# One decoder kernel, stage cross0: bf16 pairs for the norms' sums, split by POOL, and another order of its projections

## The reference, cut to what matters

```python
def rmsnorm(x, g, eps=EPS):
    var = jnp.mean(jnp.square(x), axis=-1, keepdims=True)
    return x * jax.lax.rsqrt(var + eps) * g
```

## Time and profile before

| what | before |
|---|---|
| median of 3 runs | 2926.01 us (2922.60 to 2928.53) |
| the profiled execution | 2923.55 us |
| its span | 2921.70 us |
| granted TensorE clock, mean | 0.945 |
| PE busy | 2509.2 us (86% of the span) |
| DVE busy | 1862.7 us (64%) |
| ACT busy | 1572.5 us (54%) |
| POOL busy | 864.7 us (30%) |

### The profile page before, as it was taken

One profiled execution on the slowest core, in us unless ns is written; L12 is line 12 of the kernel. 1 busy time (PEld: TensorE's weight loads), 2 busy tenths in 40 slices (PEclk: granted clock), 3 DMA queues, 4 the chain that ended last, 5 costly groups with the idle time before them and its releaser, 6 DMA issues. The chain is left out here.

```text
span 2921.7 us, 60581 instructions
## 1 busy us (share of the span) xinstructions
PE 2509.2 (86%) x21768; PEld 1612.3 (55%) x21768; DVE 1862.7 (64%) x3317; ACT 1572.5 (54%) x2742; POOL 864.7 (30%) x741
## 2 busy tenths in 40 slices
PE   6888888888888898888978999989999999986454
PEld 4555555455655565566455666655566666643222
DVE  4666663366665666666155666651688888858886
ACT  4666663176766666666043555550577777732321
POOL 4556555400110010012232212223100000146675
PEclk9999998999999999999988999999999999998777
DMA  3333333144444444446230333341477777852000
GB/s 96 71 71 92 68 73 81 47 89 92 97 95 91 95 91 96 93 94 124 80 151 21 85 88 87 88 94 46 84 146 145 143 151 145 153 115 77 20 0 29
DMA packets 752867, 263.39 MB, mean 90 GB/s; under 512 B 724816, under 2 KB 724816, under 8 KB 751184
## 3 DMA queue, kind: packets, MB, share of 16 engines
q1 hardware_dynamic: 750960, 255.48, 41.0%
q0 software_dynamic: 1760, 5.77, 0.7%
HBM read 82.84 MB, written 2.10 MB: 29 GB/s over the span
## 5 line engine op out<-in xcount | busy, mean ns | idle before, releaser
L786 ACT ACTIVATE ph<-p,ri 128x1024 bf16<-128x1024 f32 (+4 forms) x512 | 437.4, 854 | 461.6 <-DVE ri L1056 394.9
L1066 DVE SCALAR_TENSOR_TENSOR pl<-p,ri,ph 128x1024 bf16<-128x1024 f32 (+4 forms) x512 | 517.4, 1010 | 129.6 <-issue 83.5
L1122 PE MATMUL ps<-wo_hi,v_hi 128*128 128x128 bf16 x2688 | 487.2, 222 | 79.4 <-DMA wo_lo<-pl 79.3
L1123 PE MATMUL ps<-wo_lo,v_hi 128*128 128x128 bf16 x2688 | 487.0, 222 | 0.0
L1124 PE MATMUL ps<-wo_hi,v_lo 128*128 128x128 bf16 x2688 | 486.9, 222 | 0.0
L797 ACT ACTIVATE p<-p,nb 128x1024 f32<-128x1024 f32 (+4 forms) x512 | 435.7, 851 | 48.4 <-DVE nb L1049 33.9
L1122 PEld LDWEIGHTS ps<-wo_hi,v_hi 128*128 128x128 bf16 x2688 | 266.7, 99 | 142.9 <-DMA wo_lo<-pl 96.0
L1122 PE MATMUL ps<-k_hi,q_hi 128*128 128x512 bf16 (+3 forms) x768 | 277.2, 361 | 45.9 <-issue 30.1
L1123 PEld LDWEIGHTS ps<-wo_lo,v_hi 128*128 128x128 bf16 x2688 | 266.9, 99 | 39.1 <-issue 0.8
L1124 PE MATMUL ps<-k_hi,q_lo 128*128 128x512 bf16 (+3 forms) x768 | 277.1, 361 | 0.0
L1123 PE MATMUL ps<-k_lo,q_hi 128*128 128x512 bf16 (+3 forms) x768 | 276.9, 361 | 0.0
(11 more groups left out here) (197 smaller groups left out, 6066.4 us busy)
## 6 DMA issues: line engine op xcount, KB each, us to landing
raw_kv<-in_wkvself SPq DMA_DIRECT2D x32, 512.0 KB, 3.9
raw_q<-in_wqself SPq DMA_DIRECT2D x32, 256.0 KB, 2.7
wo_hi<-ph SPq DMA_TRANSPOSE x512, 3.1
wo_lo<-pl SPq DMA_TRANSPOSE x512, 3.1
raw_q<-in_woself SPq DMA_DIRECT2D x32, 256.0 KB, 2.8
raw_q<-in_wqcross SPq DMA_DIRECT2D x32, 256.0 KB, 2.7
raw_q<-in_wocross SPq DMA_DIRECT2D x32, 256.0 KB, 3.0
raw_kv<-in_wkvcross SPq DMA_DIRECT2D x24, 256.0 KB, 3.1
```

Of the source, the lines that this page charges most:

```text
L786: nc.scalar.activation(m["ph"][:, qt % 2, 0:w], m["p"][:, qt % 2, 0:w], ACT.Copy, scale=ri[:, qt % 2:qt % 2 + 1]).then_inc(p_norm, 1)
L1066: nc.vector.scalar_tensor_tensor(out=m["pl"][:, qt % 2, 0:w], in0=m["p"][:, qt % 2, 0:w], scalar=ri[:, qt % 2:qt % 2 + 1], in1=m["ph"][:, ...
L1122: nc.tensor.matmul(o, l(0), r(0), start=first, stop=False)
L1123: nc.tensor.matmul(o, l(0), r(1), start=False, stop=False)
```

## The change

1. The plan of jobs: K0 | K1, KN0 | Q, KN1 | QN, V0, V1, where it was K0 | KN0, K1 | KN1, Q | QN, V0, V1.
2. POOL splits each square into a bf16 pair `sqs` (`split_squares`: a rounding, then a subtraction), and the sums become bf16 matmuls over both halves with `onesb`. ACT waits for POOL's subtraction before it overwrites `sq`; POOL waits for the sum that read the pair before.
3. VectorE copies QN's sums directly behind the scores of step 3, ahead of the remainder; the head's output comes behind the jobs' rows on both ACT and VectorE.
4. ACT makes the key norms in step 3 between the wait for that step's scores and its exponential, where it made them at the end of step 2.

```diff
@@ Layer.jobs
-            plan = [[("K", 0)], [("KN", 0), ("K", 1)], [("KN", 1), ("Q", 0)], [("QN", 0), ("V", 0), ("V", 1)]]
+            plan = [[("K", 0)], [("K", 1), ("KN", 0)], [("Q", 0), ("KN", 1)], [("QN", 0), ("V", 0), ("V", 1)]]
@@ POOL
+                def split_squares(n, it, qt, jobs):
+
+                    for kind, half in jobs:
+                        if kind not in ("K", "Q"):
+                            continue
+                        s = 2 if kind == "Q" else half
+                        count = lambda n: c["sq"] + 3 * (n + 1) + s + 1
+                        pool.wait_ge(sq_ok, at(count, n, it))
+                        if n >= 0 or s:
+                            pool.wait_ge(job_mm, at(lambda n: c["job"] + squares_free(n, s), n, it))
+                        pool.nop(nofuse=True)
+                        nc.gpsimd.tensor_scalar(m["sqs"][0][:, :], m["sq"][:, :], 1.0, 1.0, ALU.mult, ALU.mult).then_inc(sq_hi, 1)
+                        pool.wait_ge(sq_hi, at(count, n, it))
+                        pool.nop(nofuse=True)
+                        nc.gpsimd.tensor_tensor(m["sqs"][1][:, :], m["sq"][:, :], m["sqs"][0][:, :], ALU.subtract).then_inc(sq_lo, 1)
+
+                def squares_free(n, s):
+
+                    return L.before(n - 1, 3) + 1 if s == 0 else L.before(n, 1) + 2 if s == 1 else L.before(n, 2) + 2
@@ POOL unit
                         if L.rms:
+                            split_squares(n, it, qt, L.jobs(n, qt))
                             query_norms(n, it, qt, L.jobs(n, qt))
@@ ACT job_parts
                             if L.rms:
+                                s = 2 if kind == "Q" else half
+                                act.wait_ge(sq_lo, at(lambda n: c["sq"] + 3 * (n + 1) + s, n, it))
                                 nc.scalar.activation(m["sq"][:, :], bank, ACT.Square).then_inc(sq_ok, 1)
@@ ACT unit
                         prob = m["p"][:, qt % 2, 0:L.width(qt)]
+                        if L.rms and qt == QT - 1:
+                            key_norms(n, it, qt - 1, L.jobs(n, qt - 1))
...
+                        job_parts(n, it, qt, L.jobs(n, qt))
                         if qt == QT - 1 and n:
                             heads_out(n - 1, it)
-                        job_parts(n, it, qt, L.jobs(n, qt))
                         if L.rope and qt > 0:
                             rotated(n, it, qt - 1, L.jobs(n, qt - 1))
-                        if L.rms:
-                            key_norms(n, it, qt, L.jobs(n, qt))
@@ DVE unit
                         scores(n, it, qt)
+                        job_parts(n, it, qt, L.jobs(n, qt), ("QN",))
                         if n or qt:
                             remainder(*prior)
+                        job_parts(n, it, qt, L.jobs(n, qt), ("K", "KN", "Q", "V"))
                         if qt == QT - 1 and n:
                             heads_out(n - 1, it)
-                        job_parts(n, it, qt, L.jobs(n, qt))
@@ PE job
                     elif kind == "KN":
-                        pe.wait_ge(sq_ok, at(lambda n: c["sq"] + 3 * (n + 1) + half + 1, n, it))
-                        last = nc.tensor.matmul(bank, ones[:, :], m["sq"][:, :], start=True, stop=True)
+                        pe.wait_ge(sq_lo, at(lambda n: c["sq"] + 3 * (n + 1) + half + 1, n, it))
+                        nc.tensor.matmul(bank, onesb[:, :], m["sqs"][0][:, :], start=True, stop=False)
+                        last = nc.tensor.matmul(bank, onesb[:, :], m["sqs"][1][:, :], start=False, stop=True)
                     elif kind == "QN":
-                        pe.wait_ge(sq_ok, at(lambda n: c["sq"] + 3 * (n + 1) + 3, n, it))
+                        pe.wait_ge(sq_lo, at(lambda n: c["sq"] + 3 * (n + 1) + 3, n, it))
                         for q in range(QT):
-                            last = nc.tensor.matmul(bank[:, q:q + 1], m["sq"][:, q * P:q * P + P], ones[:, 0:1], start=True, stop=True)
+                            nc.tensor.matmul(bank[:, q:q + 1], m["sqs"][0][:, q * P:q * P + P], onesb[:, 0:1], start=True, stop=False)
+                            last = nc.tensor.matmul(bank[:, q:q + 1], m["sqs"][1][:, q * P:q * P + P], onesb[:, 0:1], start=False, stop=True)
                     last.then_inc(job_mm, 1)
```

More of the change, by code:

```diff
@@ L137, in build @@
         ones = sb("ones", [P, P], F32)
+        onesb = sb("onesb", [P, P], BF16)
         idx = sb("idx", [P, IT], I32)
@@ L152, in build @@
         job_mm, job_hi, job_lo = sem("job_mm"), sem("job_hi"), sem("job_lo")
-        sq_ok, k_log, k_norm, q_norm = sem("sq_ok"), sem("k_log"), sem("k_norm"), sem("q_norm")
+        sq_ok, sq_hi, sq_lo, k_log, k_norm, q_norm = sem("sq_ok"), sem("sq_hi"), sem("sq_lo"), sem("k_log"), sem("k_norm"), sem("q_norm")
         rope_sum, rope_hi, rope_lo = sem("rope_sum"), sem("rope_hi"), sem("rope_lo")
@@ L279, in build @@
                 m["sq"] = sb("sq", [P, S], F32, s)
+                m["sqs"] = [sb(f"sq_{k}", [P, S], BF16, s) for k in hl]
                 m["rk"] = sb("rk", [P, 2, SC], F32, s)
@@ L458, in _ @@
             nc.gpsimd.tensor_scalar(idb[:, :], ident[:, :], 1.0, 1.0, ALU.mult, ALU.mult).then_inc(idb_ok, 1)
+            nc.gpsimd.tensor_scalar(onesb[:, :], ones[:, :], 1.0, 1.0, ALU.mult, ALU.mult).then_inc(idb_ok, 1)
             def split_hi(hi, src):
@@ L619, in _ @@
                     if L.rms:
+                        split_squares(-1, None, qt, L.jobs(-1, qt))
                         query_norms(-1, None, qt, L.jobs(-1, qt))
@@ L982, in _, with job_parts @@
                     continue
-                def job_parts(n, it, qt, jobs):
+                def job_parts(n, it, qt, jobs, kinds=("K", "KN", "Q", "QN", "V")):
                     u = n + 1
                     for x, (kind, half) in enumerate(jobs):
+                        if kind not in kinds:
+                            continue
                         bank = ps[:, M_BANK + (L.before(n, qt) + x) % 2, :]
@@ L1297, in unit @@
                             weigh(bn, it, bq)
+                if L.rms:
+                    pe.wait_ge(idb_ok, 2)
                 pe.wait_ge(x_lo, c["ln"] + NT)
```

## The result

The changed kernel takes 2877.65 us (median of 4 runs, 2876.55 to 2878.89) against 2924.31 us before, a ratio of 0.984 (95% interval 0.983 to 0.986): 47 us or 1.6% faster. The profiled execution has a span of 2877.1 us, 44.6 less than before. Of these, 44.4 lie between scores 0 of unit 0 and scores 0 of unit 31: 593.98 to 1328.89, 734.91 us where it was 779.35.

The account below looks back on a forecast made before the run. Bound: VectorE-ACT loop in steps 0 and 1, TensorE's V1 hole in step 3. 31 x 22.58 plus 22.0 at boundaries is 722 against 779.35, 57 less; prologue 2 more, so 55 less: 2871 us, range 2848 to 2905.

Parts of the forecast that it names:

- rk on the loop: Step 1: VectorE copies row rk after K1's low half, adding 0.61 to the two-engine loop, 5.23 instead of 4.62.
- Q behind K1's low half: Step 2: Q uses K1's bank and waits some 0.8 us on TensorE for K1's low half.
- Sum 0: First key-norm sum on TensorE: waits 1.27 us for POOL's subtraction, with 1.05 in hand before scores 2.
- QN: Q's norm sums on TensorE: wait 0.24 us for POOL, then take 0.45 as bf16 instead of 0.81.
- the hole: Step 3: TensorE's wait before V1 for nq to free QN's bank; 2.44 us a unit would go.
- The boundaries: Six loop turns: extra wait of first scores falls from 4.93 to 3.67 each, 29.6 to 22.0 us in all.
- the 1.26 in hand: End of step 3: TensorE would have the next scores 0 ready at 21.3 of 22.58 us.
- 13.9: Stage time in us put down to some nine units with the clock lowered behind the V1 wait; taken as gone.
- A: Rival: TensorE alone sets the pace, 20.06 us a unit, 128 us less, 2798; chance 5%.
- B: Rival: little gain is left, loop additions cost 1.0 to 1.8 us more per unit, 2897 to 2926; chance 14%.
- C: Rival: scattered TensorE idling lowers the clock, 24.86 us a unit, 13 us slower, 2939; chance 8%.
- splits and remainders would not meet: POOL's splits and VectorE's remainders run at different times, nothing added; if every split met one, 9 us.

Follow-up runs that it names:

- nq early: The kernel before with only VectorE's copy of QN's sums moved directly behind scores 3; 2845.3 us, ratio 0.973.
- pairs in the old plan: The kernel before with QN's sums copied directly behind scores 3 and POOL's bf16 pairs, old plan of jobs; 2882.7 us, ratio 0.987.
- new plan and head's output last: The changed kernel with ACT's key norms back at the end of step 2; 2866.6 us, ratio 0.980.
- POOL's longer split: The changed kernel with one more rounding of 0.7 us on POOL ahead of each split; 2885.6 us, ratio 0.989.
- pairs alone: The kernel before with only POOL's split and bf16 sums, old plan and old row order; 2991.9 us, ratio 1.023.
- both old: The changed kernel with QN's copy back behind the remainder and the head's output back ahead of the jobs' rows; 3038.7 us, ratio 1.040.

## Why the prediction was right

**The unit.** Forecast 4.62 + 5.23 + 5.45 + 7.28 = 22.58, measured 4.62 + 5.21 + 5.48 + 7.31 = 22.62. Each term shows in its place: rk on the loop (0.60), Q behind K1's low half (0.63 of wait, forecast some 0.8), scores 3 waiting 0.34 for TensorE, the key norms ahead of the exponential. Sum 0 waits 1.09 (forecast 1.27), QN 0.18 (0.24). QN itself was taken at 0.45 and takes 0.21; lying in TensorE's slack, that moved nothing. Walking one unit queue by queue, with pitches and not durations, gave the unit to 0.2%.

**The parts.** The units of four kernels make a ladder from before to after: nq early 23.74 to 21.28, -2.46; pairs in the old plan to 22.39, +1.11; new plan and head's output last to 21.89, -0.50; key norms late to 22.62, +0.73. The forecast had the hole at 2.44 and said that most of what TensorE gives up goes back into the loop. What it did not say, though its own terms did, is that the first edit alone would be the better kernel.

**The boundaries** are the term that was mis-sized. "At a boundary the 1.26 in hand is used first: 6 x 3.67 = 22.0": measured 28.7, 4.78 each. The slack was there and was used: from the last of the scores' matmuls to scores 0 there are 1.99 us in a plain unit and 0.95 at the boundary shown. But the 4.93 that it was taken from did not stay. In the kernel before, the second hole at the same turn was short and stood behind the scores' matmuls, where scores 0 do not wait for it:
```profile
1018.96 0.60 PE L1122 MATMUL ps<-k_hi,q_hi 128*128 128x512 bf16 x1 [3.38 <-issue]
...
1022.09 0.39 PE L1122 MATMUL ps<-cT_hi,wkv_hi 128*128 128x512 bf16 x1 [0.40 <-issue]
```
In the changed kernel it stands in front of the last of them at all six turns, and is 1.27 to 1.92 us long. Why it moved there is not known. "I take the 13.9 as gone too" was mis-sized as well. Those 13.9 were not all behind the V1 hole: of the nine long units of the kernel before, six stood right behind a boundary, and in three of the nine the low clock was what was left of the boundary's own stretch. The three inside a turn or behind the loop are gone, and the 15 units that come two or more behind a boundary stand at 22.54 to 22.62; the six right behind a boundary stay long, with 6.0 us in all. Together 12.7 us of the 12.9 by which the stage missed its 722.

**Luck.** The median came out 6.7 us above the forecast, and not 12.9, for reasons that the prediction did not have. Up to the stage's first scores the run grew by 0.8 us instead of the 2 forecast (the prologue itself, from K0's first low half on, by 0.4), what follows the stage was 1.0 us shorter, and the profiled execution of the changed kernel lies 1.2 us above its median where that of the kernel before lay 2.5 below.

**The rivals.** A (TensorE alone sets the pace, 20.06): the unit went to 22.62, and even with the hole shut and nothing added it stays at 21.19 to 21.28. B did not happen: POOL's longer split moves no unit. C did not happen in the changed kernel (0.97 granted over 600 to 1290 us, as before), but pairs alone and both old show that it can, at 0.93 and 0.90.

**POOL and VectorE.** The forecast that splits and remainders would not meet holds: all 96 subtractions of the squares take 1.15 to 1.16. Others met. The timeline of POOL in the changed unit:
```profile
1050.91 0.62 POOL L464 TENSOR_SCALAR wq_hi<-raw_q 128x512 bf16<-128x512 f32 x1
...
1059.09 1.16 POOL L598 TENSOR_TENSOR sq_lo<-sq,sq_hi 128x512 bf16<-128x512 f32 x1
...
1061.75 1.99 POOL L582 TENSOR_TENSOR nq<-nq,half_neg 128x4 f32<-128x4 f32 x1 [0.38 <-DVE nq L1028]
```
The power of nq, four elements wide, takes 1.99 us here and took 1.01 in the kernel before, where it ran beside VectorE's copy of a bank: now the remainder runs from 1061.59 for 1.27. The Trainium skill, GPSIMD Engine Reference, Key points, states that POOL contends with VectorE instructions that have two SBUF inputs, and the trace agrees for this one as well. It cost nothing, for the power is due 3.9 us later.

## What to carry to other kernels

When an engine waits for a bank, look at where the row that frees it stands in its own queue before making work cheaper: one copy of 0.16 us moved ahead of two rows gave 79 us, the whole change that contains it 47. A helper engine may take over work only with its latency in hand at the consumer: the same pairs cost 1.1 us a unit where the sum was due at once and saved 0.4 where one or two other jobs stood between. And an edit that looks free because another one made room should be timed alone: the key norms' new place cost 0.73 a unit.

## What the runs showed of the hardware that was not expected

- A remainder on VectorE took 1.58 us instead of 1.28 when a rounding on POOL, started 0.11 earlier (1050.91 beside 1051.02), ran with it: the contention goes both ways. In seven units of the changed kernel it is these 0.30, in seven more about 0.42, once 0.97 (2.25 at 1312.38, beside a subtraction that started with it); for POOL up to 0.98. In the kernel before, all remainders of the stage took 1.28 to 1.29.
- TensorE's loop turn costs more than its hole: 3.0 us without instructions, a second hole of 1.27 some 2.3 us later, and the 1.2 GHz level over the matmuls between. Written out, cross0 with its 32 units was 37 us (changed) and 46 us (nq early) shorter; the other attention stages, written out all together, gained nothing.
- A bf16 weight load of 128 x 128 with a matmul of one column behind it has a pitch of 0.026 us (eight in 0.21), half of the 0.056 of a load and a matmul with 128 columns, from which the estimate of 0.45 was made.
- Whether the clock falls behind a hole depends on more than the hole: one of 2.2 to 2.3 us, the same in every unit, was followed by a fall in six of 31 units before, and one of 2.5 us in most units of pairs alone, where three smaller waits of TensorE stand in front of it. With 4.4 to 4.7 us (both old) it fell in every unit.
